# Cross-attention: one PSUM bank given from the transposed scores to the scores, four and two in place of three and three

## The reference

```
q = proj(Wq, bq, query).reshape(b, HD, H, n)      # n = 512, H = 16, HD = 16
k = proj(Wk, bk, key).reshape(b, HD, H, n)
v = proj(Wv, bv, value).reshape(b, HD, H, n)
q, k = rotary(q), rotary(k)
scores = jnp.einsum('bdhn,bdhm->bhnm', q, k) / sqrt(HD)
prob = softmax(scores, axis=-1)
x = jnp.einsum('bhnm,bdhm->bdhn', prob, v)
out = jnp.einsum('oi,bin->bon', Wm, x.reshape(b, d_model, n)) + bm
x = x + out
```

## Time and profile before

| | us |
|---|---|
| median of 3 runs | 1784.39 (1781.94 to 1784.56) |
| the profiled execution | 1797.91 |
| its span, first to last instruction | 1796.0 |
| cross-attention in it, 426.9 to 1006.5 | 579.6 |

### The profile page before, as it was taken

The page is one execution under the profiler, slowest core; times in us unless marked ns, Lnnn a source line. Parts: engine busy times, 40 slices in busy tenths (PEclk is TensorE's granted clock), DMA queues, the critical chain, the costliest instruction groups (busy, mean ns, idle before and its releaser), DMA issues. The chain is left out here.

```text
span 1796.0 us, 28480 instructions
## 1 busy us (share of the span) xinstructions
PE 1473.7 (82%) x9504; PEld 694.0 (39%) x9521; DVE 1036.9 (58%) x1787; ACT 620.4 (35%) x1107; POOL 692.5 (39%) x707
## 2 busy tenths in 40 slices
PE   4689999884688888888888594388999999999887
PEld 2355545440122222222222351145555555556433
DVE  6446465566687878877886562023454544534476
ACT  4242404141475665665757540111111111111111
POOL 1000001145743444444301237403655646646474
PEclk9899999885599999999999687599999999999999
DMA  5862537213811312311200135306664656653465
GB/s 210 247 185 87 155 116 229 87 49 70 238 43 37 71 30 42 71 31 30 60 1 1 51 133 202 140 12 178 174 185 136 173 148 174 169 162 87 126 193 174
DMA packets 197159, 211.25 MB, mean 118 GB/s; under 512 B 90000, under 2 KB 162256, under 8 KB 196688
## 3 DMA queue, kind: packets, MB, share of 16 engines
q1 hardware_dynamic: 167696, 123.67, 26.4%
q0 software_dynamic: 18592, 66.99, 12.0%
q10 hardware_dynamic: 10784, 19.47, 2.9%
HBM read 101.09 MB, written 88.87 MB: 106 GB/s over the span
## 5 line engine op out<-in xcount | busy, mean ns | idle before, releaser
L1035 DVE TENSOR_REDUCE ca_mx<-ca_sc 128x1 f32<-128x512 f32 x512 | 326.0, 678 | 114.1 <-PE ca_sc L947 113.7
L78 PE MATMUL re_ab<-fx_w,re_xt 128*128 x1800 | 297.8, 316 | 13.2 <-DMA re_xt<-slot_rows 12.4
L1177 ACT ACTIVATE ca_pt<-ca_st 128x512 f32<-128x512 f32 x512 | 264.6, 595 | 114.4 <-PE ca_st L959 114.3
L947 PE MATMUL ca_sc<-ca_ks,ca_qs 48*128 48x512 f16 x512 | 183.9, 412 | 43.5 <-DMA ca_ks<-ca_scratch 23.3
L78 PEld LDWEIGHTS re_ab<-fx_w,re_xt 128*128 128x128 f16 x1800 | 174.2, 99 | 112.4 <-issue 15.8
L959 PE MATMUL ca_st<-ca_qs,ca_ks 49*128 49x512 f16 x512 | 171.5, 393 | 50.3 <-ACT ca_pt L1177 41.8
L78 PE MATMUL sh_ab<-fx_xn,sh_pair 128*128 (+3 forms) x576 | 139.1, 398 | 61.2 <-issue 34.8
L78 PE MATMUL re_yp<-fx_w,re_ht 128*128 (+1 forms) x666 | 156.0, 379 | 0.0
L1758 POOL TENSOR_TENSOR fx_w<-re_raw_w,fx_w 128x272 f16<-128x272 f32 x224 | 153.9, 724 | 1.7
L972 PE MATMUL ca_pv<-ca_pt,ca_va 128*32 128x512 f32 x1024 | 143.1, 624 | 1.0 <-DVE ca_turned L1044 0.5
L959 PEld LDWEIGHTS ca_st<-ca_qs,ca_ks 49*128 49x128 f16 x512 | 42.2, 94 | 244.6 <-ACT ca_pt L1177 153.9
(11 more groups left out here) (241 smaller groups left out, 2350.8 us busy)
## 6 DMA issues: line engine op xcount, KB each, us to landing
re_raw_w<-in_we POOLq DMA_DIRECT2D x56, 544.0 KB, 4.6
slot_rows<-sa_zeros SPq DMA_DIRECT2D x12, 1792.0 KB, 15.9
slot_outs<-re_ys ACTq DMA_DIRECT2D x74, 256.0 KB, 2.0
sa_scratch<-home SPq DMA_DIRECT2D x16, 512.0 KB, 3.7
ca_scratch<-ca_qk SPq DMA_DIRECT2D x64, 128.0 KB, 1.8
sa_qs<-sa_scratch SPq DMA_DIRECT2D x12, 512.0 KB, 6.8
sa_ks<-sa_scratch SPq DMA_DIRECT2D x12, 512.0 KB, 6.7
ca_qs<-ca_scratch SPq DMA_DIRECT2D x48, 128.0 KB, 3.9
```

The source lines that it names most:

```text
L78: last = nc.tensor.matmul(out, lhs(a, c), rhs(b, c), start=(m == 0), stop=(m == total - 1), skip_group_check=parts > 1)
L947: nc.tensor.matmul(sc[:, m % RING, :], qs[rows, c % SLOTS, pair, qt * P:(qt + 1) * P], ks[rows, c % SLOTS, pair, :], start=True, stop=True ...
L1035: nc.vector.reduce_max(mx[:, qd // 4, qd % 4, 2 * a + jj:2 * a + jj + 1], sc[:, m % RING, :], AX.X).then_inc(maxed, 1)
L1177: nc.scalar.activation(pt[:, (4 * qd + k) % 8, :], st[:, m % RING, :], ACT.Exp, scale=SCALE).then_inc(exp_done, 1)
```

## The change

`RING = 3` for both kinds of tile becomes `SCORES = 4` for the scores and `TURNED = 2` for the transposed scores. A score tile then waits for the maximum four tiles before it, a transposed tile for the exponential two tiles before it. No instruction is added, removed or moved on any engine; the banks and what a matmul waits for are all that changes. The sum stays at eight banks.

```diff
-    RING, ROWS = 3, 3 * XHD
+    SCORES, TURNED, ROWS = 4, 2, 3 * XHD
...
-        sc = pb("sc", [P, RING, G], F32)
-        st = pb("st", [P, RING, G], F32)
+        sc = pb("sc", [P, SCORES, G], F32)
+        st = pb("st", [P, TURNED, G], F32)
...
             def score(c, qd, k):
-                if m >= RING:
-                    pe.wait_ge(maxed, m - RING + 1)
+                if m >= SCORES:
+                    pe.wait_ge(maxed, m - SCORES + 1)
                 rows = slice(64 * (k % 2), 64 * (k % 2) + ROWS)
-                nc.tensor.matmul(sc[:, m % RING, :], qs[rows, c % SLOTS, pair, qt * P:(qt + 1) * P],
+                nc.tensor.matmul(sc[:, m % SCORES, :], qs[rows, c % SLOTS, pair, qt * P:(qt + 1) * P],
...
             def transposed_score(b, qd, k):
-                if m >= RING:
-                    pe.wait_ge(exp_done, m - RING + 1)
+                if m >= TURNED:
+                    pe.wait_ge(exp_done, m - TURNED + 1)
...
-                nc.tensor.matmul(st[:, m % RING, :], ks[rows, b % SLOTS, pair, kt * P:(kt + 1) * P],
+                nc.tensor.matmul(st[:, m % TURNED, :], ks[rows, b % SLOTS, pair, kt * P:(kt + 1) * P],
```

More of the change, by code:

```diff
@@ L1034, in maximum @@
                 dve.wait_ge(score_done[a], m // 2 + 1)
-                nc.vector.reduce_max(mx[:, qd // 4, qd % 4, 2 * a + jj:2 * a + jj + 1], sc[:, m % RING, :], AX.X
+                nc.vector.reduce_max(mx[:, qd // 4, qd % 4, 2 * a + jj:2 * a + jj + 1], sc[:, m % SCORES, :], AX.X
                                      ).then_inc(maxed, 1)
@@ L1176, in exponent @@
                     act.wait_ge(pv_done, QUADS * b + qd - 1)
-                nc.scalar.activation(pt[:, (4 * qd + k) % 8, :], st[:, m % RING, :], ACT.Exp, scale=SCALE
+                nc.scalar.activation(pt[:, (4 * qd + k) % 8, :], st[:, m % TURNED, :], ACT.Exp, scale=SCALE
                                      ).then_inc(exp_done, 1)
```

## The result

The changed kernel takes 1811.17 us, median of four runs (1808.99 to 1816.3), against 1784.47 of the kernel before beside it (1781.94 to 1790.75). The ratio is 1.0143, with an interval of 1.0115 to 1.017: slower by 26.7 us. The forecast was slower by 40.8.

The account below looks back on a forecast made before the run. TensorE together with the round trip to ScalarE was taken to set the period. Mixed turns 33.6 plus last turn 7.2 gave 40.8 us, on the 1784.39 median 1825.2; the range was 1806 to 1843.

Parts of the forecast that it names:

- The last turn: Turn that only attends: 15 blocks of transposed scores pay 0.49 each, less 0.2 already waited, 7.2 us.
- The mixed turns: Seven turns that attend one batch and take the next one's maxima: 4.8 us slower each, 33.6 in all.
- The step: In each quad without cover, tile 3 and all TensorE work behind it start 0.49 later, nothing inside the quad hiding it.
- Quads 2 to 4: In a mixed turn these pay nothing, beneath output-projection waits of 1.27 for GpSimd and 1.66 for VectorE.
- my one walked turn: One mixed turn, 637 to 706, walked quad by quad with other engines' pieces unchanged; its 4.8 taken seven times.
- Quads 11 and 12: In a mixed turn these pay nothing, since TensorE waits until 679.25 for VectorE to empty the projection's bank.
- rival 2: In the mixed turns the clock falls more often: 10 to 20 us more, 1835 to 1845; chance 15%.
- The fourth score bank: TensorE's 19.8 us of waits for maxima bound its gain; taken as 0 beyond 0.2 a mixed turn.
- rival 3: Fourth score bank wins: all 19.8 us of maxima waits go, transposed waits hide beneath VectorE, 1772; chance 4%.
- Turn -1: First turn taking maxima, without transposed scores: no gain from the fourth score bank, 0.
- Rival 1: VectorE is the pacemaker and covers the step except in about five quads a mixed turn: 24 us, 1809; chance 15%.
- The sign that I had set for it: A mixed turn under 71 us, where 73.7 was forecast, would show Rival 1.

Follow-up runs that it names:

- e12: Changed kernel, four score and two transposed banks, but with all six for the transposed tiles of the last turn: 1756.17 us, ratio 1.0098 to the kernel before.
- e2: The changed kernel again, four score and two transposed banks, beside its variants on another chip: 1772.28 us, ratio 1.0178 to the kernel before.
- e1: Kernel before with three score banks, two transposed banks and one bank left empty: 1784.43 us, ratio 1.0257.
- e8: Kernel before, three and three banks, with VectorE's maximum over 128 of 512 columns (result no longer the reference's): 1691.69 us, ratio 0.9701.
- e9: Changed kernel, four and two banks, with the maximum over 128 of 512 columns: 1749.72 us, ratio 1.0051 to the kernel before.
- e5: As e1, plus two unread matmuls into the empty bank before every third transposed tile of the last turn: 1819.56 us, ratio 1.0175 to the kernel before.
- e11: As e10, plus the three score banks also used for transposed tiles in the last turn: 1711.74 us, ratio 0.982 to the kernel before.
- e6: Kernel before, three and three banks, with every side job moved in front of the block's fourth pair of tiles: 1774.61 us, ratio 0.9902.
- e10: Kernel before with only projections, values and quad 7's transpose moved in front of the fourth pair of tiles: 1714.44 us, ratio 0.9823.
- e7: Changed kernel, four and two banks, with every side job moved in front of the third pair: 1810.82 us, ratio 1.0115 to the kernel before.

## Why the prediction was right or wrong

Right in sign and within its range (1806 to 1843), with the mechanism it named; too high by 14 us in size. Point by point:

- **The last turn, +7.2.** Right: +6.7 over the 15 quads and +7.7 to the table load, with tiles at 1.07 and 0.48 behind that. e12 gives this turn six banks and takes the loss away, and 3.9 more, so the loss hangs on the banks. The price was met in an execution without a fall of the clock; e2 and e1, with one, show +11.7 and +16.6 over the 15 quads, for which my sum had no term.
- **The mixed turns, +33.6.** Here the sum failed: +22.3. The step is the claim that everything behind tile 2 "starts 0.49 later" and "Nothing hides that inside the quad". Averages over turns 1 to 4, each quad from the first transposed tile of its block to that of the next:

| quads | forecast | measured |
|---|---|---|
| 15, 0, 1 | +1.5 | +0.98 |
| 2, 3, 4 | 0 | +0.91 |
| 5 | +0.1 | +0.36 |
| 6, 7 | +1.0 | +0.96 |
| 8, 9 | +0.68 | +0.59 |
| 10 | +0.5 | +0.11 |
| 11, 12 | 0 | -1.61 |
| 13, 14 | +1.0 | +1.17 |
| sum | +4.8 | +3.5 |

  In quads 15, 0 and 1 the wait for the maximum hid 0.13 and more, as the row at 690.70 shows and e8 and e9 bear out. Quads 2 to 4 were right and the clock hides it: turns 1 and 5, with as many output projections at the lower level before as after, have 0.00 and -0.01 there, and turns 3 and 4, with one more, have +1.67 and +1.68. Quad 10 is a matter of counting: after the change the first tile of its block itself waits 0.30 for an exponential, where it waited for nothing before, and that part of the step falls into quad 9. So quads 8 to 10 belong together: +0.70 where I had 1.18, and +1.30 with the short maximum, so VectorE covered 0.6 there. Turns 0, 5 and 6 lack another 6 us against my one walked turn, turn 6 (+1.7) most: it projects nothing, and my walk was of a turn that does.
- **Quads 11 and 12, "nothing".** They gave back 1.6. VectorE in order of time, before and then after:

```profile
678.08 0.78 DVE L1040 TENSOR_SCALAR ca_nm<-ca_mx 128x16 f16<-128x16 f32 x1
```
```profile
683.04 0.12 DVE L1040 TENSOR_SCALAR ca_nm<-ca_mx 128x16 f16<-128x16 f32 x1
683.08 0.41 DVE L1064 TENSOR_TENSOR ca_va<-ca_proj,home 128x256 f32<-128x256 f32 x1
...
684.72 1.03 DVE L1052 TENSOR_TENSOR ca_quot<-ca_turned,ca_rden 128x256 f32<-128x256 f32 x1
```

  and GpSimd's pass on `ca_xn`, before and then after:

```profile
677.68 2.27 POOL L1222 TENSOR_TENSOR ca_xn<-ca_norm,ca_xn 128x512 f16<-128x512 f32 x2 [1.03 <-ACT ca_xn L1138]
```
```profile
683.20 2.27 POOL L1222 TENSOR_TENSOR ca_xn<-ca_norm,ca_xn 128x512 f16<-128x512 f32 x2 [1.60 <-ACT ca_xn L1138]
```

  Before, that pass was running when VectorE came to its tiny row, which took 0.78; after, it starts behind it, and the row takes 0.12, in each of turns 0 to 4. That is 0.66 less on VectorE's unbroken row of work up to the values, and 0.63 more came from the clock (values in 0.83, not 1.46); the rest of the 1.6 I can't place. The 0.66 isn't a gain of the whole turn: the pass now meets VectorE's division, a few rows later, which takes 1.03 where it took 0.40, and that falls behind the values, into quads 12 and 13. A walk that keeps "pieces as long as the trace has them" can't see any of this. That the meeting is the cause wasn't tried by itself, but all 14 traces agree: the 398 tiny rows with no GpSimd pass beside them took 0.12 to 0.17, the 50 with one 0.17 to 1.28.
- **The clock, rival 2 (15%).** In the mixed turns, where I had put it, it is there and cancels: output projections at the lower level cost 1.69 more in each of turns 3 and 4, and the values of quad 12 give back 0.63 in each of turns 0 to 4, under 1 us net. That it cancels is luck, since my sum had a term for neither. In the last turn, of which I had said that short waits don't bring a fall, rival 2 is partly true. Waits of 0.47 a quad didn't come with a fall; waits of 0.69 did in e1 and e2 and not in the profiled execution of the change, and filled with work (e5) the clock held in the one trace. The Trainium skill ("TensorE: Matmul & The Clock Gate", section "A second HAM failure mode: psum-queue depth-cycling") says that short idle times between groups of matmuls, as a kernel goes round its PSUM banks, can be frequent enough to make the clock swing. The trace of e2 agrees, with its 2.88 and then 4.18 a quad; that the bank waits are the cause isn't shown, since e11 has a fall behind another wait.
- **The fourth score bank, 0, and rival 3 (the bank wins, 4%).** Of the 19.8 us of waits for maxima, 17 vanished, and in mixed turns 1 to 5 nothing came of it (e1 beside e2). Turn -1 I had wrongly dismissed: it is 2.9 us shorter after the change, and 4.4 between e1 and e2. In quad 12 I had the second wait growing by the whole 1.52 of the first, and it grew by 0.52. So the bank's worth is some 5 us (4.4 in turn -1 and 2.1 in turn 6, less 0.8 in turn 0 and 0.5 in the five turns between), and not 19.8 nor 0.
- **Rival 1 (VectorE covers it, 1809, 15%).** In size it was nearer than my forecast: it gave the mixed turns 17, I gave 33.6, and they have 22.3. In its reason it is right for a part. VectorE's load does cover 2.4 us a turn (e8 beside e9), which I had put at nothing outside quads 4, 5, 8, 9, 11 and 12. But it isn't the pacemaker: the quads in which it isn't late pay 0.36 to 0.58 each, and with its load cut the price rises to 5.6 a turn, above my 4.8. The sign that I had set for it, a mixed turn under 71, is nearly there: turn 2 takes 71.39, between that and the 73.7 forecast.

Open: what lets the clock fall in one execution and not in another, and where the last 0.3 us of quads 11 and 12 come from.

## What to carry to other kernels

A ring of PSUM banks costs what its round trip costs: with one bank less, each group pays one more piece of the engine that empties it, but only as far as no other ring's wait lies beside it, so write down every wait of the group, paired instructions too, before pricing one. Where a bank wait can't be shortened, put work that is surely ready into it (e6 and e10, 1.0 and 1.8% faster with the banks as they were). Work that itself waits holds up what stands behind it (e7); whether it is better left where it was, these runs don't settle. A stage whose last part uses only one of the rings can lend it the idle banks of the other (e12). Before a difference of one quad or one turn is put down to a change, the same instruction's length at the two clock levels has to be looked up in both traces: it hid a right forecast in quads 2 to 4 here.

## What the runs showed of the hardware that was not expected

- In the last turn with two transposed banks, TensorE idle for 0.69 in each period of 2.88, the granted clock fell to the 1.2 GHz level in four of five traces (e1, e2, e7 and e9, not the first of the changed kernel). With three transposed banks, idle for 0.47 in 2.39, it fell during the 15 quads in none of five. The fall lengthened the quads by 1.3 each, more than twice the 0.49 that the bank itself cost. In e5, 0.60 of unneeded matmuls a quad, 9 us in all, lengthened no quad, and the clock stayed at 1.00 in its one trace.
- A VectorE row of 128 x 16 took 0.78 while a GpSimd pass of 128 x 512 was running and 0.12 when none was; VectorE's division of 128 x 256 took 1.03 and 0.40. Moving the meeting moved the loss from one row to the other.
